# Causal mask products in the rounded float format instead of bfloat16

## The reference, cut to what matters

```python
scores = jnp.einsum('bnth,bnsh->bnts', q, k) * (1.0 / math.sqrt(h))
causal = jnp.tril(jnp.ones((T, T), dtype=bool))
scores = jnp.where(causal, scores, -jnp.inf)
attn = jax.nn.softmax(scores, axis=-1)
...
scores = jnp.where(causal[None, None, :, :], scores, jnp.float32(-1e+30))
probs = jax.nn.softmax(scores, axis=-1)
```

## Time and profile before

| what | value |
|---|---|
| time, median of 3 runs | 1503.41 us (1501.34 to 1503.43) |
| the profiled execution: its own time | 1503.67 us |
| its span, first to last instruction | 1501.4 us |
| PE busy | 1395.1 us, 93% of the span |
| PEld busy | 1209.9 us, 81% |
| DVE, ACT, POOL busy | 1006.8, 710.6, 464.4 us |
| mean granted TensorE clock | 0.969 of full speed |
| mask products L1583, L1842 | 128 and 128 matmuls |

### The profile page before, as it was taken

The page is one execution under the profiler, slowest core; times in us unless marked ns, Lnnn a source line. Parts: engine busy times, 40 slices in busy tenths (PEclk is TensorE's granted clock), DMA queues, the critical chain, the costliest instruction groups (busy, mean ns, idle before and its releaser), DMA issues.

```text
span 1501.4 us, 25866 instructions
## 1 busy us (share of the span) xinstructions
PE 1395.1 (93%) x9284; PEld 1209.9 (81%) x9284; DVE 1006.8 (67%) x1821; ACT 710.6 (47%) x1856; POOL 464.4 (31%) x360
## 2 busy tenths in 40 slices
PE   3999999799999796989999999999999999948998
PEld 2878888567777575879999999999999999837887
DVE  7666666679999734466667766677666776664554
ACT  3666666622222222246556665556555565422332
POOL 5211111122321741425344442525243444124000
PEclk9999999999999897899999999999999999979999
DMA  6101020232230001111212121101102020010000
GB/s 210 30 1 30 2 72 6 80 106 84 84 119 0 22 1 45 36 36 29 71 29 70 28 70 28 62 9 41 56 28 70 28 70 28 1 63 8 15 14 28
DMA packets 39685, 67.90 MB, mean 45 GB/s; under 512 B 4940, under 2 KB 13799, under 8 KB 39618
## 3 DMA queue, kind: packets, MB, share of 16 engines
q1 hardware_dynamic: 37522, 65.69, 13.7%
q10 hardware_dynamic: 2096, 1.33, 0.3%
HBM read 60.68 MB, written 2.13 MB: 42 GB/s over the span
## 4 chain that ended last, share of the span: by engine, by line
PE 87%; DVE 7%; ACT 2%; issue 1%; DMA 1%; POOL 0%; SPq 0%; DVEq 0%; POOLq 0%; ACTq 0%
PE PS L348 21%; PE PS L350 20%; PE PS L349 20%; PE PS L1568 3%; PE PS L1866 3%; PE PS L1852 2%; PE PS L1851 2%; PE PS L1853 2%; PE PS L1501 2%; PE PS L1587 2%; PE PS L1549 1%; PE PS L1521 1%; DVE ln_xn L935 1%; PE PS L1842 1%; PE PS L1583 1%
## 5 line engine op out<-in xcount | busy, mean ns | idle before, releaser
L348 PE MATMUL PS<-XNH,E_WL 128*128 128x256 f32 x768 | 214.9, 280 | 0.8 <-DVEq L343 0.8
L350 PE MATMUL PS<-XNH,E_WH 128*128 128x256 f32 x768 | 214.7, 280 | 0.0
L349 PE MATMUL PS<-XNL,E_WH 128*128 128x256 f32 x768 | 214.0, 279 | 0.0
L553 POOL TENSOR_TENSOR E_sw<-E_sw,rope2s 128x1024 f32<-128x1024 f32 x64 | 104.5, 1633 | 274.2 <-ACT E_sw L605 274.2
L1277 DVE TENSOR_REDUCE E_nb<-PS 128x4 f32<-128x512 f32 x64 | 61.3, 958 | 178.6 <-PE PS L1853 178.6
L605 ACT ACTIVATE E_sw<-PS 64x256 f32<-64x256 f32 (+1 forms) x128 | 89.5, 700 | 120.7 <-PE PS L350 119.2
L348 PEld LDWEIGHTS PS<-XNH,E_WL 128*128 128x128 f32 x768 | 144.5, 188 | 2.4 <-DVEq L343 1.2
L349 PEld LDWEIGHTS PS<-XNL,E_WH 128*128 128x128 f32 x768 | 144.5, 188 | 1.2
L350 PEld LDWEIGHTS PS<-XNH,E_WH 128*128 128x128 f32 x768 | 144.3, 188 | 0.0
L463 POOL TENSOR_TENSOR E_WL<-raw,E_WH 128x512 fp32r<-128x512 f32 x80 | 110.0, 1404 | 106.7 <-ACT E_WH L605 106.2
L801 ACT ACTIVATE E_p<-PS,E_nb 128x128 f32<-128x128 f32 (+1 forms) x256 | 104.3, 420 | 34.5 <-DVE E_nb L1277 34.5
(11 more groups left out here) (272 smaller groups left out, 4036.3 us busy)
## 6 DMA issues: line engine op xcount, KB each, us to landing
raw<-in_w SPq DMA_DIRECT2D x104, 256.0 KB, 2.7
words<-in_words SPq DMA_DIRECT2D x11, 768.0 KB, 4.2
wo<-in_wo SPq DMA_DIRECT2D x32, 256.0 KB, 3.7
zb<-z_scratch SPq DMA_DIRECT2D x11, 384.0 KB, 4.9
scb<-in_scales SPq DMA_DIRECT2D x11, 384.0 KB, 5.5
X<-in_x SPq DMA_DIRECT2D x8, 256.0 KB, 6.0
SGH<-XNH SPq DMA_DIRECT2D x8, 256.0 KB, 2.7
SGL<-XNL SPq DMA_DIRECT2D x8, 256.0 KB, 2.8
```

The lines of the kernel that those rows point to most:

```text
L348: nc.tensor.matmul(o, sl, mh, start=first, stop=False, **shared)
L349: nc.tensor.matmul(o, sh, ml, start=False, stop=False, **shared)
L350: return nc.tensor.matmul(o, sh, mh, start=False, stop=last, **shared)
L553: nc.gpsimd.tensor_tensor(E_sw[:, heads, :], E_sw[:, heads, :], rope2s[:, :].unsqueeze(1).broadcast_to([P, heads.stop - heads.start, SEQ]) ...
```

## The change

Both mask products become products in the rounded float format, like the products around them. The two bfloat16 constants and their DMAs go. In their place DVE forms two 128x128 tiles once, from constants that are there already: `identr`, a rounded copy of `ident`, and `hidden`, 2^100 where hidden and else 0, from `mask01`. The operands also trade places: `hidden` is now stationary and the unit matrix moves. PE waits once, before the first scores, for the two tiles (`a["mask"]`). The two DVE instructions stand before `zeros_plus_one(0)` in DVE's program order.

```diff
-        identb = keep("identb", [P, P], BF16)
-        mask_ts = keep("mask_ts", [P, P], BF16)
+        identr = keep("identr", [P, P], F32R)
+        hidden = keep("hidden", [P, P], F32R)
...
-            consts = [(ident, "ident"), (identb, "identb"), (mask_ts, "mask_ts"), (mask01, "mask01"), (shift_k, "shift_k"), (rope0c, "rope0c"), (rope0s, "rope0s"),
+            consts = [(ident, "ident"), (mask01, "mask01"), (shift_k, "shift_k"), (rope0c, "rope0c"), (rope0s, "rope0s"),
...
-            dve.wait_ge(const_in, 16 * 9)
+            dve.wait_ge(const_in, 16 * 7)
+            V.tensor_copy(identr[:, :], ident[:, :]).then_inc(a["mask"], 1)
+            V.tensor_scalar(hidden[:, :], mask01[:, :], -2.0 ** 100, 2.0 ** 100, ALU.mult, ALU.add).then_inc(a["mask"], 1)
...
-                    mm(seen, identb[:, :], mask_ts[:, :].unsqueeze(1).broadcast_to([P, 2, P]), start=True, stop=False, skip_group_check=True)
+                    mm(seen, hidden[:, :], identr[:, :].unsqueeze(1).broadcast_to([P, 2, P]), start=True, stop=False, skip_group_check=True)
...
+            pe.wait_ge(a["mask"], 2)
             scores(0, 0)
...
-                            mm(seen, identb[:, :], mask_ts[:, :].unsqueeze(1).broadcast_to([P, 2, P]), start=True, stop=False,
+                            mm(seen, hidden[:, :], identr[:, :].unsqueeze(1).broadcast_to([P, 2, P]), start=True, stop=False,
```

More of the change, by code:

```diff
@@ L276, in sems @@
             return {n: sem(f"{prefix}_{n}") for n in names.split()}
-        a = sems("a", "stage0 stage1 init proj t1 t2 q hi lo tp ev vps vcp sc least exp rec pt pe pd pv inv rt r ot wo_ps x")
+        a = sems("a", "mask stage0 stage1 init proj t1 t2 q hi lo tp ev vps vcp sc least exp rec pt pe pd pv inv rt r ot wo_ps x")
         def prepared(b, g, ago=0):
@@ L474, in _ @@
             rests0(range(8, 12))
-            pool.wait_ge(const_in, 16 * 9)
+            pool.wait_ge(const_in, 16 * 7)
             def rotate(unit):
@@ L1461, in dense_tile @@
                 last.then_inc(ffn_ps, 1)
-            pe.wait_ge(const_in, 16 * 9)
+            pe.wait_ge(const_in, 16 * 7)
             normalise(0)
@@ L2020 @@
     sin2 = np.concatenate([-np.sin(t2), np.sin(t2)], 1)
-    bf16 = mybir.dt.np(mybir.dt.bfloat16)
     turned = np.array([-0.25, 1.0], f32)[:, None, None, None]
@@ L2040 @@
         sc3=rows(a["L3_ffn_scale"][:, 0]), b3=rows(a["L3_ffn_bias"]),
-        ident=np.eye(P, dtype=f32), identb=np.eye(P, dtype=bf16), mask_ts=hidden.astype(bf16),
+        ident=np.eye(P, dtype=f32),
         mask01=(hidden.T == 0).astype(f32),
```

## The result

| kernel | median of 7 runs, us | runs |
|---|---|---|
| before | 1503.21 | 1501.34 to 1504.02 |
| changed | 1508.63 | 1507.72 to 1514.6 |

The ratio is 1.0046, its 95% interval 1.0031 to 1.006: slower by 4.7 to 9.0 us, by 5.4 between the medians. The profiled execution of the changed kernel took 1514.3 us (span 1512.0), near the upper end of its runs, so its span may not be set against that of before as it stands.

What follows compares the result with a forecast made beforehand. PE alone was taken to set the time in both attention stages. Terms 0.7 + 2.5 + 1.9 - 0.2 = +4.9 us on the profiled 1503.67 gave 1508.6, forecast as a median of 1508.3 us, range 1504.9 to 1511.0.

Steps and rivals of the forecast that it cites:

- layer 2: 32 slots of four mask products: rounded costs 0.015 to 0.03 us more a slot, 31 on the path, 0.7 us.
- layer 0: 64 groups of two mask products: 1.85 us open plus 0.75 covered, less 0.1 swallowed by waits, 2.5 us.
- start: Two added DVE instructions before `zeros_plus_one(0)` each wait for a POOL product: +1.9 us, bounds 0 and 2.9.
- two DMAs less: Before the work begins, two DMAs of 32 KB go: -0.2 us, with 0 and -0.5 as ends.
- no load gap means no gain: Layer 2 group: bfloat16 delays a load 0.12 us, yet five rounded products take 0.585 or 0.60 us against 0.57.
- in the open: 17 layer 0 groups behind a change of tile shape, weight load uncovered: 0.44 us against 0.32, together 1.85 us.
- Covered: 47 layer 0 groups behind full-array work, weight load hidden: +0.016 us each, together 0.75 us.
- The 0.2 us for half clock: At the start, the delayed second projection falls wholly in a half-clock stretch: some +0.2 us, within the 1.9.
- The start is covered: Rival, chance 0.17: DVE's copies of 128 columns slip between POOL's products, the start costs 0: 1506.4 us.
- All loads in the open: Rival, chance 0.03: every rounded mask load or product pays in full, 256 x 0.11 = 28 us: 1531 us.
- faster: Rival, chance 0.03: layer 2 saves the delayed load 32 times, 3.8 us; layer 0 and start free: 1499.4 us.
- By the clock: Rival, chance 0.12: both half-clock stretches in layer 0 turns vanish, 3.3 us less, not slower: 1505.0 us.

Runs made afterwards that it cites:

- the later profile: The unchanged changed kernel profiled again, beside the kernel before: 1507.69 us against 1502.97.
- the later two: The kernel before, unchanged, profiled twice more: 1504.02 and 1504.33 us.
- the two kernels on the start: Kernel before with only the two DVE instructions added: 1504.74 us, ratio 1.001, start 18.97; changed kernel with them moved later: 1506.7 us, 1.0015, start 17.47.
- two instructions later: The changed kernel with its two DVE instructions moved some 15 us later, where POOL is short of work: 1506.7 us, ratio 1.0015 to the kernel before.

## Why the prediction was right, by its own steps

| term | predicted, us | measured, us |
|---|---|---|
| layer 2 | 0.7 (0.5 to 0.9) | 0.6 to 0.7, by the groups and by the slots |
| layer 0 | 2.5 | 2.6 (0 half-clock stretches against 0), 2.5 to 2.7 (2 against 2) |
| start | 1.9 (0 to 2.9) | 1.5 to the second projection; to the first mask product 1.4, at like clock |
| two DMAs less | -0.2 (-0.5 to 0) | not resolved: PE's first instruction starts at 16.8 to 18.2 us in the 8 profiles with the two DMAs there and at 17.0 to 17.7 in the 4 without |
| sum | 4.9 | 4.5 to 4.9 without the DMAs; the runs gave 5.4 between the medians, with 4.7 to 9.0 as interval |

The terms as measured, about 4.7 us, lie at the low end of the runs' interval. If the whole is dearer than that, no stage of these traces shows by what; the rest is put down to the clock (below), which is argued and not shown.

*Layer 2* went as told: the gap in front of the group closes, the rounded products start 116 to 122 ns apart where the third and the fourth bfloat16 one started 109 ns after the one before, and the second change outweighs the first, by 18 to 23 ns a group. That no load gap means no gain was the step that decided the sign here.

*Layer 0, in the open.* Told: load and product 0.23 us, then 0.21. Measured over the 15 groups behind the products with the values: 224 and 211 ns (222 and 210 in the later profile), before 120 and 203. From the last product with the values to the scores, the unchanged neighbours, it is 636 ns against 527: +0.109 us, as told. With the 2 groups behind score products, 17 x 0.109 = 1.9. *Covered.* Told +0.016 for 47 groups; measured +0.020 for 44 of them. The other 3 follow the 12 transposes directly and were not told apart: there the distance grew from 421 to 516 ns, nearly as if in the open, 0.3 us in all. Why a full-array transpose does not cover the load there is open. Gross that is 1.9 + 0.9 + 0.3 = 3.1 us, of which 2.6 reached the end. So 0.5 us were swallowed, by waits behind if the argument of the prediction holds, which had taken off 0.1; no trace was read for where. The gross sum was told too small and the swallowing too, and that the two misses cancel is luck. What would have been seen was also told wrong for the covered groups: 0.33 us from mask to score products, where the records show 0.41 to 0.42, for the reason given above.

By the Trainium skill ("TensorE: Matmul & The Clock Gate", Weight-path perf modes — Fast Weight Load (FWL) and DoubleRow) the 17 open loads were 1.6 us, an estimate; the runs give 1.9. It rests on the page's rule for a plain load, 128 / 1.2 = 107 ns (there under LDWEIGHTS), and on 32 cycles for a fast one, which the page gives as the theory for fp8 weights. With the factor of about 2 that it calls measured for the fast load the estimate would be 17 x 107 / 2 = 0.9 us. In the records the loads of the mask tiles last 98 ns in bfloat16 and 188 to 190 rounded, so the factor is borne out, but the 17 open groups cost twice that second estimate: here the measurement decides.

*The start.* The mechanism was right and the term too large. Played through, the second projection was to come 1.7 us later; it came 1.5 later, as POOL's fourth product ended at 35.15 and L970 at 35.43, not at 35.7, with L972 at once behind it. The 0.2 us for half clock were not a cost of the change. The 12 products of the second projection take 1.70 us from first to last start in the first profile of before, and 2.51 to 2.52 in all eleven others, with either kind of masks. So the first profile of before alone had the full clock there. From PE's first instruction to the first mask product it took 31.99 us, the later two 32.8, and the changed kernel 34.2 both times: 1.4 us at like clock, 2.2 against that one profile. The copy, which takes 0.245 us by itself, ends 0.08 us after POOL's first product. DVE's work hangs on POOL's, product by product. Of the rule that the prediction drew from the Trainium skill ("SBUF — State Buffer", Who interferes with whom), the two kernels with and without the instructions in that place are the test, and they agree with it: 18.97 and 17.47 us. The prediction stretched it in one point: the rule for a two-port mode is for operations with one input, like the copy, L970 and L972. L966 reads two tensors in SBUF, which the same section names as a case of its own, beside a GpSimd instruction that reads SBUF; its 1.69 and 1.76 us agree with that.

*The rivals.* "The start is covered" fell with the two kernels on the start. "All loads in the open" and "faster" fell with the timelines. "By the clock" stands as what spreads the runs, not as an effect of the change. Among the 25 runs of the kernel before beside "two instructions later", the two with the highest mean granted clock (0.973) took 1499.9 and 1501.5 us, the two with the lowest (0.965 and 0.966) 1509.2 and 1509.4. Among kernels with bfloat16 masks the turns had 0, 1 or 2 half-clock stretches, with 235.0, 236.5 and 238.0 us, so one costs 1.5 us (told: at most 1.65); rounded masks had 0 or 2, with 237.6 and 240.7.

The first profile of the changed kernel had a span 10.6 us longer than that of before, 5.9 more than the terms explain. By stages: 3.3 us lie in the output projection of layer 0, which fell in a half-clock stretch (below), 0.6 are the clock in the start, 0.5 lie in layer 1, 1.3 are the other pace in layer 2 (31 x 0.043), and 0.9 a half-clock stretch at 680 us; 0.8 came back near 1320 us. Windows of that execution, columns as in the earlier trace rows:
```profile
304.70:311.30 6.60, 6.07 (x7) 2.52 (x8) 0.38 (x1) 0.00 (x0) 0.00 (x0) 0.50 0.00 0
690.00:1290.00 600.00, 600.00 (x4230) 556.53 (x4230) 410.18 (x722) 355.84 (x887) 243.17 (x162) 1.00 0.15 45
```
and of the later profile of the same kernel, a window in the same products:
```profile
307.50:309.00 1.50, 1.50 (x4) 0.59 (x4) 0.00 (x0) 0.00 (x0) 0.00 (x0) 1.00 0.00 0
```
These products of 512 columns start every 0.85 us in the half-clock window and every 0.43 us at full clock. What makes the granted clock fall in one execution and not in the next was not found; what the change itself does to it, if anything, stays open.

## What to carry to other kernels

Price a change of format from start to start, between neighbours that stay the same on both sides: the records of the changed product itself gave 0.273 against 0.282 us in layer 2, and in layer 0 the distance from mask to scores grew from 0.31 to 0.42 where the cost was 0.02. Ask for each place whether the weight load has a matmul of the same shape to hide behind; 17 places of 96 without such cover made half of PE's loss before waits, 1.9 of 3.8 us. Such cover has to be read for each kind of neighbour: 3 groups behind full-array transposes paid 0.095 us each all the same. A short one-time instruction is not short where another engine holds what it needs, and 0.3% is found by stages, with the totals only as a check.

## What was not expected of the hardware

- A bfloat16 weight load behind rounded products starts only when the product before it is through, and still costs next to nothing: the whole layer 2 group is 18 to 23 ns shorter than with rounded loads that start early.
- The same instructions in layer 2 run at two paces, 20.767 and 20.810 us a slot, in different executions of one unchanged kernel, at a granted clock of 1.00. It shows in work that the change does not touch, the score products and the products with the values, and these can go separately, the one slow and the other quick. The cause is open.
- DVE operations of 128 and of 512 columns, in three number formats, take nearly the same 1.3 to 1.8 us beside POOL's products of 512 columns, with DMAs running or not: POOL's product sets the time, not the operation. Operations that read PSUM took their usual 0.4 to 0.5 us beside the same products.
